# Last layer's attention: the inverse row sums are spread over the partitions by transfers through DRAM

## The reference

```python
def step(h, p):
    op = jnp.argmax(h[0, 0, :NOPS])
    q = h @ p['wq'][op]
    k = h @ p['wk'][op]
    v = h @ p['wv'][op]
    attn = jax.nn.softmax(jnp.einsum('bqd,bkd->bqk', q, k) * scale, axis=-1)
    y = jnp.einsum('bqk,bkd->bqd', attn, v) @ p['wo'][op]
    h = jnp.where(p['am'][op], y, h)
    z = jax.nn.relu(h @ p['w1'][op] + p['b1'][op]) @ p['w2'][op] + p['b2'][op]
    h = jnp.where(p['fm'][op], z, h)
    return (h, None)
```

## Time and profile before

| | before |
|---|---|
| median of three runs | 709.54 us |
| the profiled execution | 711.64 us, span 709.8 us |
| third layer's attention, from TensorE's first inverse matmul (L292, block 0) to its last value product (block 15) | 600.15 to 688.10 us of the span |
| one block in the steady part | 6.08 us |
| last feed-forward | 688.10 us to the end |

### The profile page before, as it was taken

The page is one execution under the profiler, slowest core; times in us unless marked ns, Lnnn a source line. Parts: engine busy times, 40 slices in busy tenths (PEclk is TensorE's granted clock), DMA queues, the critical chain, the costliest instruction groups (busy, mean ns, idle before and its releaser), DMA issues.

```text
span 709.8 us, 10911 instructions
## 1 busy us (share of the span) xinstructions
PE 618.5 (87%) x3732; PEld 267.0 (38%) x3732; DVE 581.7 (82%) x622; ACT 415.2 (59%) x643; POOL 451.1 (64%) x240
## 2 busy tenths in 40 slices
PE   8889879889877888988878887988979999999996
PEld 3323222222222212222222222345756446777771
DVE  5799999999999999999999999364365457788755
ACT  4878777668567566766774663353445525544441
POOL 7599999999999999999999999510000220000002
PEclk9989999999999999989999999999899999999999
DMA  3876679686666675666666763000000000000001
GB/s 104 220 267 211 230 227 291 226 259 226 232 232 253 211 250 211 236 217 210 234 233 222 234 241 115 1 1 0 3 5 8 1 20 1 1 2 1 2 2 65
DMA packets 32107, 101.20 MB, mean 143 GB/s; under 512 B 6821, under 2 KB 7342, under 8 KB 32046
## 3 DMA queue, kind: packets, MB, share of 16 engines
q1 hardware_dynamic: 30486, 99.42, 41.6%
q10 hardware_dynamic: 1240, 0.88, 0.4%
q0 software_dynamic: 320, 0.13, 0.1%
HBM read 94.64 MB, written 2.10 MB: 136 GB/s over the span
## 4 chain that ended last, share of the span: by engine, by line
PE 44%; DVE 23%; issue 19%; ACT 7%; POOL 5%; DMA 1%; DVEq 0%; ACTq 0%; POOLq 0%
DVE hh_all L1641 9%; DVE pb L1636 8%; PE py L279 7%; PE pb L242 6%; PE px L302 5%; PE py L816 5%; POOL hc L1956 4%; PE pb L1044 2%; PE py L1068 2%; PE px L845 2%; PE pb L804 2%; POOL dbu L1967 2%; PE px L292 1%; DVE dtu_all L1615 1%; PE px L763 1%
## 5 line engine op out<-in xcount | busy, mean ns | idle before, releaser
L1956 POOL TENSOR_TENSOR hc<-hh_all,cc 128x1024 f32<-128x1024 f32 x128 | 298.5, 2355 | 6.3 <-DVE hh_all L1641 4.6
L1641 DVE TENSOR_TENSOR_SCAN hh_all<-da,pb 128x1024 f32<-128x1024 f32 x80 | 182.9, 2286 | 3.4 <-ACT da L1324 0.4
L1970 POOL TENSOR_TENSOR yg<-w_xs 128x512 f32<-128x512 f32 x10 | 12.6, 1266 | 227.1 <-DVE w_xs L1783 132.7
L816 PE MATMUL py<-hc,w_cst 64*64 64x512 f32 x1024 | 148.2, 639 | 8.5 <-DVE yg L1652 8.5
L1967 POOL TENSOR_TENSOR dbu<-bb,dtu_all 128x1024 f32<-128x1024 f32 x48 | 113.2, 2358 | 5.0 <-DMA bb<-scr 5.0
L1641 DVE TENSOR_TENSOR_SCAN hh_all<-pb,dbu 128x1024 f32<-128x1024 f32 x48 | 108.9, 2269 | 2.0 <-DVE dtu_all L1615 1.7
L1636 DVE TENSOR_TENSOR pb<-pb,dtu_all 128x1024 f32<-128x1024 f32 x80 | 97.1, 1214 | 3.7 <-PE pb L804 1.2
L804 PE MATMUL pb<-bc,w_sel 128*128 128x512 bf16 x160 | 51.8, 408 | 53.1 <-DVE hh_all L1641 53.0
L1324 ACT ACTIVATE da<-dt_all,w_aneg 128x1024 f32<-128x1024 f32 x80 | 89.8, 1138 | 2.7 <-DVE dt_all L1622 1.8
L1324 ACT ACTIVATE pb<-dt_all,w_aneg 128x1024 f32<-128x1024 f32 x48 | 53.6, 1116 | 64.3 <-DVE hh_all L1641 63.8
L816 PEld LDWEIGHTS py<-hc,w_cst 64*64 64x64 f32 x1024 | 31.2, 136 | 80.9 <-issue 54.4
(11 more groups left out here) (326 smaller groups left out, 1020.0 us busy)
## 6 DMA issues: line engine op xcount, KB each, us to landing
cc<-scr SPq DMA_DIRECT2D x128, 512.0 KB, 4.3
bb<-scr SPq DMA_DIRECT2D x48, 512.0 KB, 5.0
w_xs<-w_xm SPq DMA_DIRECT2D x8, 256.0 KB, 6.5
w_xs<-hc SPq DMA_DIRECT2D x6, 256.0 KB, 3.8
scr<-bcf SPq DMA_DIRECT2D x8, 128.0 KB, 4.6
out<-yg SPq DMA_DIRECT2D x4, 256.0 KB, 2.6
w_xst<-in_x SPq DMA_DIRECT2D x1, 512.0 KB, 4.6
w_cst<-in_consts ACTq DMA_DIRECT2D x1, 404.0 KB, 5.0
```

The source lines that it names most:

```text
L816: last = nc.tensor.matmul(py[part(t), half(r)], ident[part(r), part(r)], hc[u % NHC][part(r), half(t)], start=(n == 0), stop=(n == NS - 1) ...
L1641: nc.vector.tensor_tensor_scan(hh[u % NHH][:, :], decay[:, :], drive[:, :], 0.0, ALU.mult, ALU.add).then_inc(scan_done, 1)
L1956: nc.gpsimd.tensor_tensor(hc[u % NHC][:, :], hh[u % NHH][:, :], cc[u % NCC][:, :], ALU.mult).then_inc(hc_done, 1)
```

## The change

TensorE's two small matmuls (L292) and ScalarE's copy (L416) are gone for the third layer; the second layer keeps them. In their place GpSimd runs `spread_inverse` for every block: it waits for the reciprocal, writes `rc` (128 x 2 numbers of 4 bytes) transposed to two rows in DRAM, waits until that has landed, and loads each row, repeated over 64 partitions, to one of four slots of `rs`. VectorE's `output` now waits for the values and for both loads; its reciprocal of block g waits for the loads of block g-2, since it overwrites what they were made from.

```diff
     def output(self, dve, k, g, to):
 
-        dve.wait_ge(self.rb_out, self.GRP * k + g + 1)
-        self.nc.vector.tensor_tensor(to, (self.ob, self.rb)[g % 2][:, 0:128], self.rs[:, g % 2, :], ALU.mult).then_inc(self.o_out, 1)
+        if self.causal:
+            dve.wait_ge(self.rb_out, g + 1)
+        else:
+            dve.wait_ge(self.o_full, self.GRP * k + g + 1)
+            dve.wait_ge(self.rs_in, 32 * (self.GRP * (k - 1) + g + 1))
+        self.nc.vector.tensor_tensor(to, (self.ob, self.rb)[g % 2][:, 0:128], self.rs[:, g % (2 if self.causal else 4), :],
+                                     ALU.mult).then_inc(self.o_out, 1)
+
+    def spread_inverse(self, pool, k, g, scr, passed):
+
+        at = self.GRP * k + g
+        row = scr[g % 2, 2 * (g // 2 % 2):2 * (g // 2 % 2) + 2, 0:128]
+        pool.wait_ge(self.o_out, at - 3)
+        settle(pool, self.rc_done, at + 1, passed)
+        pool.dma_start(row.rearrange("r q -> q r"), self.rc[:, 2 * (g % 2):2 * (g % 2) + 2],
+                       allow_slow_non_contiguous=True).then_inc(self.rc_out, 16)
+        settle(pool, self.rc_out, 16 * (self.GRP * (k - 1) + g + 1), passed)
+        for r in range(2):
+            pool.dma_start(self.rs[C * r:C * r + C, g % 4, :], row[r:r + 1, :].broadcast_to((C, 128))).then_inc(self.rs_in, 16)
@@ pe_values
-        pe.wait_ge(self.rc_done, self.GRP * k + g + 1)
+        if self.causal:
+            pe.wait_ge(self.rc_done, g + 1)
         atleast(pe, self.o_out, self.GRP * k + g - 1)
-        for r in range(2):
+        for r in range(2 if self.causal else 0):
             i = 2 * (g % 2) + r
             nc.tensor.matmul(bank[C * r:C * r + C, 128:256], self.rc[:, i:i + 1].broadcast_to((128, C)),
@@ dve_inverse
-        atleast(dve, self.o_full, self.GRP * k + g - 1)
+        if self.causal:
+            atleast(dve, self.o_full, g - 1)
+        elif g >= 2:
+            dve.wait_ge(self.rs_in, 32 * (self.GRP * (k - 1) + g - 1))
@@ act_all
-            if g >= 2:
-                self.act_inverse(act, k, g - 2)
         self.act_turned(act, k, self.GRP - 1)
-        self.act_inverse(act, k, self.GRP - 2)
-        self.act_inverse(act, k, self.GRP - 1)
@@ pool_attend
-            pass
+            for g in range(GRP):
+                ea.spread_inverse(pool, k, g, scr, passed)
```

More of the change, by code:

```diff
@@ L82, in __init__ @@
         self.rc_done, self.o_full, self.o_out = sem("rc_done"), sem("o_full"), sem("o_out")
-        self.rb_out = sem("rb_out")
+        if causal:
+            self.rb_out = sem("rb_out")
+        else:
+            self.rc_out, self.rs_in = sem("rc_out"), sem("rs_in")
     def prime(self, eng, *counts):
@@ L95, in prime_act @@
     def prime_act(self, act):
-        for sem, count in ((self.q_out, 2), (self.fold_act, 2), (self.v_act, 2), (self.p_done, 2 * self.GRP), (self.pts_act, self.GRP), (self.rb_out, self.GRP)):
+        for sem, count in ((self.q_out, 2), (self.fold_act, 2), (self.v_act, 2), (self.p_done, 2 * self.GRP), (self.pts_act, self.GRP)):
             act.sem_inc(sem, count)
@@ L563, in build_all @@
         x_in = [sem(f"x_in{p}") for p in range(2)]
-        scaled, turned, turn_out, s_spread, vec_used = sem("scaled"), sem("turned"), sem("turn_out"), sem("s_spread"), sem("vec_used")
+        scaled, turned, turn_out, s_spread = sem("scaled"), sem("turned"), sem("turn_out"), sem("s_spread")
         a_exp, stats_done, aggr_done, pair_done, gn_chain = (
@@ L631, in build_all @@
         LN3 = 2 * NCH
-        ea = Attention(nc, ctx, w, False, {**bufs, "kt": hn})
+        ea = Attention(nc, ctx, w, False, {**bufs, "kt": hn, "rs": small[:, 512:1024].rearrange("p (a q) -> p a q", a=4)})
         store = hc[0]
```

## The result

The changed kernel takes 767.92 us (median of 4 runs, 767.44 to 768.91), the kernel before 710.14 us beside it (4 runs, 708.71 to 711.5). The ratio is 1.083, 95% interval 1.081 to 1.085: the change costs 58 us. I had forecast 706.3 us in a range of 704.2 to 711.5, so both the size and the sign were wrong.

What follows compares the result with a forecast made beforehand. The prediction took TensorE as the bound of the third layer's attention: 4.10 us saved by the removal, less 0.9 lost at the bare end, gave -3.2 us, so 706.3 us for the median, range 704.2 to 711.5.

Steps and rivals of the forecast that it cites:

- W: Landing time of GpSimd's write to DRAM in each block: between 2.1 and 4.8 us, taken as 3.2.
- the quiet rows: Transfers on another queue in the quiet part, used to bound landings: 2.1 us for small-piece loads, 2.6 for a store.
- P: Time GpSimd needs for one block, write, landing and two loads: 4.5 us, ends 3.4 and 6.3.
- L: Latency from VectorE's reciprocal to the spread inverse's arrival: 6.7 us, ends 4.9 and 9.5.
- the free 5.8: At the end of the attention, latency up to 5.8 us after block 15's reciprocal costs nothing; any excess goes one to one.
- rival 3: In the loop, GpSimd becomes the bound and blocks fall behind from 5.82 us each: +6.8 us, 716.3 us; chance 0.13.
- the forecast's own case: End of the attention partly bare, loop hidden: 705.2 to 707.6 us, own range 705.0 to 707.8; chance 0.50.
- The removal: TensorE's inverse matmuls gone: 0.26 us in each of 14 loop blocks, 0.24 and 0.22 behind, 4.10 us saved.
- rival 4: In the loop, a second chain as long keeps the block at 6.08 us: 710.0 us; chance 0.05.
- VectorE's added waits: One more wait at reciprocal and output, some hundredths each, hidden by 1.09 us idle; up to 1.6 us uncovered.
- The bare end: After block 15's reciprocal, latency beyond the free length delays the feed-forward's relu: 0.9 us lost, 0.3 allowed for VectorE's passing.
- the signs named ahead: Profile checks: steady block 5.82 us if right; reciprocal or output waiting for DMA, GpSimd's blocks over 5.8 apart, if GpSimd binds.

Runs made afterwards that it cites:

- experiment 2: Changed kernel, but blocks 1 to 15 write two whole 512-byte rows of a constant instead of 256 4-byte pieces, same waits and loads: 708.38 us, ratio 0.997.
- experiment 3: Changed kernel, but blocks 1 to 15 load 256 pieces of 4 bytes from DRAM to a spare tile in place of the write: 709.1 us, ratio 1.000.
- experiment 1: Changed kernel, but blocks 1 to 15 leave out the inverse spreading altogether (no matmul, copy or transfer; stale numbers used): 706.7 us, ratio 0.996.
- experiment 11: Changed kernel, but blocks 0 to 13 write with 4-byte gaps that VectorE skips, and 14 and 15 use TensorE and ScalarE: 706.67 us, ratio 0.995.
- experiment 7: Changed kernel, but blocks 1 to 15 write each 4-byte piece into its own 64 bytes of DRAM, loads fetching block 0's rows: 707.97 us, ratio 1.000.
- experiment 6: Changed kernel, but blocks 1 to 15 write the same 1 KB as 128 adjacent pieces of 8 bytes, loads fetching mixed rows: 713.1 us, ratio 1.006.
- experiment 9: Changed kernel, but blocks 1 to 15 write 256 4-byte pieces 8 bytes apart, loads fetching block 0's rows: 713.17 us, ratio 1.003.
- experiment 5: Changed kernel, but only image 0's column is written, 128 pieces of 4 bytes, image 1's row stale: 760.41 us, ratio 1.071.
- experiment 10: Changed kernel, but consecutive queries land 64 bytes apart at the same density, one write per image, output reading them back in order: 762.57 us, ratio 1.073.
- experiment 4: Changed kernel, but the 256-piece write goes out on SyncE's queue without waiting; GpSimd waits for it and loads: 779.47 us, ratio 1.099.
- experiment 8: Changed kernel, but only even blocks 0 to 12 go through DRAM, the nine others by TensorE and ScalarE: 710.71 us, ratio 1.002.

## Why the prediction was wrong

The failed step is the landing of the write, W. The prediction put it "between 2.1 and 4.8 us", took 3.2 because the DMA engines are nearly idle here and so "nearer to the quiet rows", and measured from the start of the issue it is 0.74 + 7.49 = 8.2. The rows I bounded it with are loads of small pieces and stores of large ones; none was a write of small pieces to DRAM. Experiments 2 and 3 show that each of the two neighbours was a fair price for itself (2.7 us with its issue for whole rows, 3.2 for a load of 256 pieces), and neither for the thing in question. I had called the 256 pieces unseen and looked for their price in GpSimd's software, which is 0.2 us. The bound was drawn from the nearest rows as if nearest meant an end.

With W = 8.2 the prediction's own sum comes close. Its formula gives P = 0.1 + 8.2 + 0.1 + 1.06 = 9.46; the trace has 9.29, without the 0.1 us that I allowed for each semaphore. With 9.29 each block falls behind by 3.47 us over 5.82, in 15 blocks 52.1 us. L becomes 0.1 + 8.2 + 0.1 + 0.53 + 2.9 (the loads' landing in the page after) = 11.8, 6.0 over the free 5.8. Less the 4.10 saved that is +54.0 to the relu, with P = 9.46 it is +56.5; measured +53.8. That the first fits to 0.2 us is partly luck. With the measured 5.86 us a block, 3.5 saved and 5.4 free (below) it is 51.5 + 6.4 - 3.5 = +54.4: three errors of 0.4 to 0.6 us nearly cancel. Behind it come the 4.8 us of the last stretch that the sum didn't have. This is the mechanism of rival 3, with its place, its threshold and its carrying over; only its size was wrong, +6.8 us where 58 were measured, since it was priced at W = 4.8. One of its figures was also summed wrongly: for W just at 4.7 the formulas give P = 5.96, 2.1 us in 15 blocks, 2.4 at the end and +0.4 in all, not +3. And L from 5.8 to 7.8 gives 705.4 to 707.4 us for the forecast's own case, where the text has 705.2 to 707.6 and 705.0 to 707.8.

The other steps:
- The removal. 0.22 us a block, not 0.26 (experiment 1, 11), because the distance of starts of L292 and the values (0.26) isn't what the loop gives back: the values' own stretch grew by 0.04. For 16 blocks that is 3.5 of the 4.1 us. No second chain took over, so rival 4 is refuted by experiment 1.
- VectorE's added waits are hidden once nothing is late: 5.86 us a block with them (experiments 2, 7, 11) and without.
- The bare end. The free length was 5.4 us, not 5.8 (experiment 2), since VectorE's passing to the feed-forward is 0.65 us, not 0.3.
- The clock was not in the sum at all. The wait of 10.02 us was followed by the lower level and cost 2.7 us in the last stretch; waits of 1.91 and 1.43 us at the same place (experiments 6 and 9) did the same. No row of before could have shown it, but each rival with waits of some microseconds should have carried a term for it. Nor was the +2.1 us behind VectorE's last instruction.
- Of the signs named ahead, those of rival 3 were the ones to be seen: reciprocals waiting for a DMA, GpSimd's blocks 9.29 us apart.
- The Trainium skill's read, change and write back of transfers under 512 bytes (page DMA: Bandwidth & Descriptors, Specifications) was cited as speaking for rival 3 "without a size", and the range left that case out. The measurements agree with it in direction (whole rows of 512 bytes 2.2 us, pieces of 4 bytes side by side 7.5), but its threshold alone doesn't give the price: pieces of the same 4 bytes waited 2.1 us in experiment 7 and 7.4 in experiment 5.

That pieces close together are merged one after another by the memory is my reading of experiments 5, 6, 7, 9 and 10 and of the DMA engines that move nothing; no run shows it. Shown is that the wait depends on the places, and that number and order of the pieces and the queue matter little. The exact length of the stretch is open: 64 bytes is the unit of my layouts, and 512 bytes would order the five the same way.

## What to carry to other kernels

A wait for a landing is a term of its own. If no row shows that kind of transfer (direction, size of piece and distance between pieces), its upper end is open, and the range must reach to where the chain behind it would put the time. When numbers go from partitions to a row by way of DRAM, leave gaps between them and let the engine that reads them skip the gaps (in this kernel worth 0.5%, experiment 11, where the dense write cost 8.3%). Don't take engines that move nothing for free ones, and don't put another transfer behind such a write, if it is waited for. At the end of a stage, where nothing hides a transfer, keep the on-chip way.

## What the runs showed that I had not expected

- 256 numbers of 4 bytes written to DRAM side by side land 7.5 us after GpSimd is through with them, and for most of that time the DMA engines move nothing; 64 bytes apart, 2.1 us. The fixed cost of about 2.0 us of the Trainium skill (page DMA: Bandwidth & Descriptors, the anatomy of one DMA on GpSimd's path) fits the second and the whole rows, not the first.
- 128 of them land no sooner than 256 (7.36 against 7.49 us).
- Two such writes in flight took 9.1 to 12.5 us from issue to the loads, and cost more than one behind the other. Loads issued behind one stood still with it: weights that land in 2.2 us landed after 11 (experiment 4).
- After waits of 4.03 us (the change) and 10.02 us TensorE went on at the 1.2 GHz level, 3.35 us for the eight score matmuls that take 1.99; 1.91 and 1.43 us at the handover were enough in experiments 6 and 9, and after 3.31 us in experiment 10 the scores at 680.20 still took 1.99. The length of one wait thus doesn't tell it.
- Behind VectorE's last instruction the span went on for 4.9 us in the kernel before, 4.7 in experiment 1, both without a transfer of GpSimd's in the attention, 5.0 with 21 of them (experiment 8), 4.5 with 32 (experiment 4, whose writes go by SyncE), 6.4 with 42 (experiment 11), 6.5 with 64 (experiment 10), and 6.5 to 7.5 with 48 (the change, experiments 2, 3, 5 to 7 and 9). From 42 transfers on that queue up, the end is thus some 2 us longer, in one profiled execution each; what causes it wasn't tried.
